# Four gated attention layers: two heads in each 64-row tile of TensorE, and value products unit by unit

## The reference

```
x = x + tanh(g_xattn[0]) * _L0_xattn_ref(_layernorm(x), ctx, ctx, ...)   # 16 heads of 8 features, biases
x = x + tanh(g_ffn[0])   * _L0_ffn_ref(_layernorm(x), ...)
x = x + tanh(g_xattn[1]) * _L1_xattn_ref(ctx, ctx, _layernorm(x), mask_Bx1xSxS2, ...)
...                                                                     # 16 heads, mask: z = where(mask == 0, -1e-20, z)
x = x + tanh(g_xattn[2]) * _L2_xattn_ref(...)                           # one head of 128 features
...
x = x + tanh(g_xattn[3]) * _L3_xattn_ref(..., mask_B, ...)              # 16 heads, only the first valid_len keys count
x = x + tanh(g_ffn[3])   * _L3_ffn_ref(_layernorm(x), ...)
```

## Time and profile before

| what | us |
| --- | --- |
| median of three runs | 6744.95 |
| the profiled execution | 6736.52 |
| its span, first to last instruction | 6734.7 |
| layer 0 attention: first product for a maximum, last update of `x` | 70.5, 1384.1 |
| layer 1 attention: last update of `x` | 3866.9 |
| layer 3 attention: last update of `x` | 6649.9 |
| TensorE busy, share of the span | 88% |

### The profile page before, as it was taken

The page is one execution under the profiler, slowest core; times in us unless marked ns, Lnnn a source line. Parts: engine busy times, 40 slices in busy tenths (PEclk is TensorE's granted clock), DMA queues, the critical chain, the costliest instruction groups (busy, mean ns, idle before and its releaser), DMA issues. The chain is left out here.

```text
span 6734.7 us, 123692 instructions
## 1 busy us (share of the span) xinstructions
PE 5947.1 (88%) x42776; PEld 4044.1 (60%) x42776; DVE 4732.6 (70%) x12652; ACT 3471.3 (52%) x5250; POOL 1972.7 (29%) x1415
## 2 busy tenths in 40 slices
PE   6999999969897999999999956768498799999996
PEld 4666666659894555555555545645388466566653
DVE  6878777867676666666666676634577777777775
ACT  3666666655553444444444433423255466666664
POOL 2222222224453222222222122334255222222220
PEclk9999999989997999999999977878699799999998
DMA  3333333220002333333333132356332333232321
GB/s 75 77 78 73 72 72 75 63 68 21 21 21 68 81 77 81 78 79 75 76 79 75 35 68 52 60 157 183 98 118 81 82 72 71 67 69 68 69 67 25
DMA packets 200964, 492.88 MB, mean 73 GB/s; under 512 B 31689, under 2 KB 135318, under 8 KB 199162
## 3 DMA queue, kind: packets, MB, share of 16 engines
q1 hardware_dynamic: 200386, 485.47, 29.5%
HBM read 270.18 MB, written 2.25 MB: 40 GB/s over the span
## 5 line engine op out<-in xcount | busy, mean ns | idle before, releaser
L850 PE MATMUL a_max<-a_stack,a_qblk 96*100 96x482 f32 (+1 forms) x4608 | 2003.5, 455 | 114.3 <-DVE a_mx L671 35.7
L550 ACT ACTIVATE a_probs<-a_scores 128x800 f32<-128x800 f32 (+1 forms) x1536 | 1281.3, 838 | 1019.0 <-PE a_scores L867 656.9
L863 PE MATMUL a_scores<-a_qblk,a_stack 128*128 128x400 f32 (+1 forms) x4608 | 1378.7, 372 | 8.1 <-POOL a_qblk L455 2.7
L665 DVE CUSTOM_DVE_ANT_0 a_dump<-a_max,a_mqf 100x482 f32<-100x482 f32 (+1 forms) x1536 | 978.5, 657 | 426.4 <-PE a_max L850 395.6
L850 PEld LDWEIGHTS a_max<-a_stack,a_qblk 96*100 96x100 f32 x4608 | 767.2, 167 | 745.1 <-issue 205.6
L671 DVE CUSTOM_DVE_ANT_0 a_dump<-a_max,a_penq 100x482 f32<-100x482 f32 (+1 forms) x1536 | 955.6, 657 | 280.9 <-PE a_max L850 261.7
L657 DVE TENSOR_REDUCE a_mx<-a_max 100x1 f32<-100x482 f32 (+1 forms) x1536 | 941.4, 654 | 257.6 <-PE a_max L850 239.8
L879 PE MATMUL a_pv<-a_probs,a_v_aug 128*32 128x200 f32 x18432 | 1051.8, 340 | 3.4 <-ACT a_probs L548 2.1
L863 PEld LDWEIGHTS a_scores<-a_qblk,a_stack 128*128 128x128 f32 (+1 forms) x4608 | 840.4, 186 | 185.6 <-issue 52.7
L1165 POOL TENSOR_TENSOR f_hb<-f_hb,f_wb 128x400 f32<-128x400 f32 x560 | 655.8, 1185 | 965.1 <-DVE f_hb L1413 490.2
L548 ACT ACTIVATE a_probs<-a_scores,a_kbias 128x800 f32<-128x800 f32 (+1 forms) x768 | 697.5, 926 | 413.6 <-PE a_scores L863 413.4
(11 more groups left out here) (302 smaller groups left out, 8471.7 us busy)
## 6 DMA issues: line engine op xcount, KB each, us to landing
a_stack<-a_khi SPq DMA_DIRECT2D x768, 180.5 KB, 3.4
a_ctxT<-in_ctxT_dram SPq DMA_DIRECT2D x128, 722.0 KB, 8.5
a_stack<-a_klo SPq DMA_DIRECT2D x384, 180.5 KB, 3.5
f_wb<-weights_by_token SPq DMA_DIRECT2D x24, 1600.0 KB, 10.7
f_wb<-weights_by_token SPq DMA_DIRECT2D x64, 400.0 KB, 6.3
a_ctxn<-in_ctxn_dram SPq DMA_DIRECT2D x32, 704.0 KB
a_mt_i<-in_mask1T_dram SPq DMA_DIRECT2D x32, 600.0 KB, 6.9
a_mq_i<-in_mask_dram SPq DMA_DIRECT2D x32, 564.1 KB
```

What stands on the lines that cost most here:

```text
L550: act.activation(out_, in_, ACT.Exp, scale=scale).then_inc(sc_free, 1)
L665: nc.vector.tensor_tensor_reduce(dump[:, k % 2, 0:n], src, mqf[:, b % 2, o:o + n], 1.0, -3.0e38, ALU.mult, ALU.max, out_).then_inc(mx_free, 1)
L850: pe.matmul(to[0:S, 0:n], qblk[0:96, b % 2, HALF * h + head, :], stack[0:96, b % 2, g, o:o + n], start=True, stop=True).then_inc(mx_full, 1)
L863: ins = pe.matmul(out_, stack[:, b % 2, 2 * h + g, kt * D:kt * D + r], qblk[:, b % 2, HALF * h + 4 * g:HALF * h + 4 * g + 4, :].rearrange( ...
```

## The change

The layout of keys and queries is new. `stack` and `qst` (in place of `qblk`) have four blocks of 32 rows. Two of them, rows 0 to 63 or 64 to 127, hold one half of the heads. A block of 32 rows is one head: rows 8 to 31 are its three parts of 8 features, rows 0 and 1 take minus the maximum in two parts, row 2 (layer 3) the penalty row for keys beyond the valid length, and the rest is ones against zeros. A product for a maximum now has 64 rows, and the scores of a unit are four products of 64 rows and 200 columns (two heads) in place of two of 128 rows and 400 columns.

`LEAD` is 24 units, one whole sample, and `half_of` swaps the halves on every second sample. So the maxima of sample b+1 and the scores of sample b always use different halves of the rows, and TensorE's list now alternates: one product for a maximum, two for scores, one for a maximum, two for scores, and then the value products of the unit before, each unit.

The key parts now go to memory (DRAM) with two DMAs a sample (`k_store`) and come back with eight. Four small DMAs a sample put the maxima into `qst` (`neg_load`). GpSimd makes the query parts with five instructions (`q_parts`) and the two parts of the maxima (`neg_parts`). In layer 3 the penalty per key is in the product, so that VectorE uses the plain reduction of layer 0 and ScalarE no bias. In layer 1 the two penalty products of a unit stand ahead of the maxima and scores. The query bias (layer 0) and a one in row 2 (layer 3) come from an added product of one row, `q_row`.

```diff
-LEAD = 16
+LEAD = UNITS
+ROWS = 32
...
+        SLOTS = 4
+        k_dram = nc.dram_tensor(f"{name}_k_parts", [SLOTS, 2, GROUPS, 2, 2, DK, KEYS], F32, kind="Internal").ap()
...
+        OUT_AT, NEG1_AT, CONCAT_AT, WO_AT, Q_AT, U_AT, NEG0_AT = 2, 4, 5, 8, 10, 13, 15
+        K0_AT, K12_AT, V01_AT, V2_AT = 1, 3, 7, 9
+        K0_FIRST, K12_FIRST, Q_FIRST, NEG_FIRST = 3, 6, 9, 14
...
+        def half_of(b, j):
+
+            return (b + j) % 2
...
+            def k_store(b):
...
+                for part, src in enumerate((khi, klo)):
+                    sp.dma_start(k_dram[b % SLOTS, :, :, :, part, :, :].rearrange("t g s i k -> (t g s) i k"),
+                                 src[:, :].bitcast(F32)).then_inc(k_out, 16)
...
+            def stack_load(b, j):
+                h = half_of(b, j)
+                sp.wait_ge(k_out, 32 * (b + 1))
+                scored(sp, b - 2, j)
+                if lens is not None and b == 0:
+                    sp.wait_ge(gone_out, 16)
+                for r in range(2):
+                    at, from_ = ROWS * (2 * h + r), k_dram[b % SLOTS, h, :, r]
+                    sp.dma_start(stack[at + 8:at + 24, b % 2, :, 0:KEYS].bitcast(F32),
+                                 from_.rearrange("g p i k -> (p i) g k")).then_inc(stack_in[b % 2][h], 16)
+                    sp.dma_start(stack[at + 24:at + 32, b % 2, :, 0:KEYS].bitcast(F32),
+                                 from_[:, 0].rearrange("g i k -> i g k")).then_inc(stack_in[b % 2][h], 16)
...
+            def neg_load(b, j):
+                h = half_of(b, j)
+                taken(sp, "neg", 2 * b + j)
+                for r in range(2):
+                    at = ROWS * (2 * h + r)
+                    sp.dma_start(qst[at:at + 2, b % 3, :, r, :].bitcast(F32), nsb[at:at + 2, :, :].bitcast(F32))\
+                      .then_inc(neg_in, 16)
...
+                act.activation(out_, in_, ACT.Exp, scale=scale).then_inc(sc_free, 1)
...
+            def q_parts(b):
+                taken(pool, "q", b)
+                scored(pool, b - 3, 1)
+                step(pool.tensor_copy(qh[:, :, :], qf[:, :, :]))
+                step(pool.tensor_scalar(ql[:, :, :], qh[:, :, :].bitcast(F32), low[:, 0:1], None, ALU.mult))
+                step(pool.tensor_tensor(ql[:, :, :], qf[:, :, :], ql[:, :, :], ALU.add))
+                for r in range(2):
+                    ins = pool.tensor_scalar(qst[:, b % 3, :, r, :], ql[:, :, :], low[:, 1 + r:2 + r], None, ALU.mult)
+                ins.then_inc(qst_ready, 1)
...
+            def neg_parts(b, j):
...
+                step(pool.tensor_copy(cols[:, :, :, 0], nm_))
+                pool.tensor_tensor(cols[:, :, :, 1], nm_, cols[:, :, :, 0].bitcast(F32),
...
+                nc.vector.tensor_copy(qf[:, :, :], p_ring("q", b)[:, 0:GROUPS * S].rearrange("p (g s) -> p g s", g=GROUPS))\
...
+                if mask is None:
                     nc.vector.tensor_reduce(out_, src, AX.X, ALU.max).then_inc(mx_free, 1)
                     return
...
+                reduce_ = nc.vector.tensor_reduce(nm[:, h, :], mx[:, h, :, :, :].rearrange("p g r c -> p (g r) c"), AX.X,
+                                                  ALU.max, negate=True)
+                reduce_.then_inc(nm_ready, 1)
...
+                nc.vector.tensor_copy(nsb[at:at + 2 * ROWS, :, :], p_ring("neg", 2 * b + j)[at:at + 2 * ROWS, 0:GROUPS * S]
+                                      .rearrange("p (g s) -> p g s", g=GROUPS)).then_inc(mx_free, 1)
...
-                    ins = pe.matmul(to[0:96, g * S:(g + 1) * S], wq[:, g, :], xnT[:, b * S:(b + 1) * S],
-                                    start=True, stop=True)
+                    ins = pe.matmul(to[:, g * S:(g + 1) * S], wq[:, g, :], xnT[:, b * S:(b + 1) * S],
+                                    start=True, stop=q_row is None)
+                    if q_row is not None:
+                        ins = pe.matmul(to[:, g * S:(g + 1) * S], q_row[:, g, :], ones_row[:, :], start=False, stop=True)
...
+                for g in range(GROUPS):
+                    ins = pe.matmul(to[at:at + 2 * ROWS, g * S:(g + 1) * S], nmsp[:, h, g, :].bitcast(F32),
+                                    ident[0:S, 0:S], start=True, stop=True)
+                ins.then_inc(mx_full, 1)
...
+                at = 2 * ROWS * half_of(b, j)
+                pe.matmul(to[0:S, 0:n], qst[at:at + 2 * ROWS, b % 3, g, r, :],
+                          stack[at:at + 2 * ROWS, b % 2, g, o:o + n], start=True, stop=True).then_inc(mx_full, 1)
...
+            def score_mm(b, u, g):
+                j, kt = divmod(u, KT)
+                if u % KT == 0 and g == 0:
+                    pe.wait_ge(neg_in, 32 * (2 * b + j + 1))
+                to = slot("exp", UNITS * b + u) if g == 0 and mask is None else p_slot("exp", UNITS * b + u)
+                at = 2 * ROWS * half_of(b, j)
+                ins = pe.matmul(to[:, g // 2, g % 2 * 2 * S:(g % 2 + 1) * 2 * S],
+                                stack[at:at + 2 * ROWS, b % 2, g, kt * D:(kt + 1) * D],
+                                qst[at:at + 2 * ROWS, b % 3, g, :, :].rearrange("p r s -> p (r s)"),
+                                start=mask is None, stop=mask is None or g % 2 == 1)
+                if g == GROUPS - 1:
+                    ins.then_inc(sc_full, 1)
...
+                for i in range(2):
+                    pe.matmul(to[:, i, 0:4 * S].rearrange("p (h s) -> p h s", h=4), identb[:, :],
+                              bc(pen[:, b % 2, u % KT, :], 1, 4), start=True, stop=False)
...
+                    if mask is not None:
+                        penalty_mm(b, u)
                     max_mm(2 * g)
-                    score_mm(b, u)
+                    score_mm(b, u, 0)
+                    score_mm(b, u, 1)
+                    max_mm(2 * g + 1)
+                    score_mm(b, u, 2)
+                    score_mm(b, u, 3)
                     if b > 0:
...
-                    max_mm(2 * g + 1)
-                    if u % 2 == 0 and (b > 0 or u > 0):
-                        for back in (2, 1):
-                            at = UNITS * b + u - back
-                            pv_mm(at // UNITS, at % UNITS)
+                    if b > 0 or u > 0:
+                        at = UNITS * b + u - 1
+                        pv_mm(at // UNITS, at % UNITS)
...
+        out = np.zeros(w.shape[:1] + (GROUPS, 4, 32), w.dtype)
+        for r in range(4):
+            for g in range(GROUPS):
+                n = HALF * (r // 2) + 2 * g + r % 2
+                head = w[:, DK * n:DK * n + DK]
+                out[:, g, r, 8:32] = np.tile(head, (1, 3))
+        return out.reshape(w.shape[:1] + (GROUPS, D))
```

372 lines of the change are left out of this document (165 added, 207 removed).

## The result

| | median | runs |
|---|---|---|
| before | 6740.3 us | 6734.5 to 6745.7 |
| after | 7052.3 us | 7025.5 to 7074.8 |

The changed kernel is slower: ratio 1.046, 95% interval 1.042 to 1.050. The forecast was 6780 us. 7052 lies in the range on record (6590 to 7120), but outside the forecast's own (to 6870), and between the forecast and rival 1; neither tells the cause. The profiled execution has a span of 7060.6 us at a mean clock of 0.884, 326 us over that of before.

What follows compares the result with a forecast made beforehand. TensorE was taken to bound all three attentions. From 6736.5 us, -35 in the steady part and +73 at the ends gave 6775 profiled, forecast as 6780; range 6590 to 7120, within full overlap 6690 to 6870.

Steps and rivals of the forecast that it cites:

- rival 1: Group of maxima and scores: halves overlap only in part, loads share one way in; 0.62 us, kernel 7115; chance 0.16.
- rivals 1 and 2: Group of maxima and scores: partial overlap (0.62 us, kernel 7115, chance 0.16) or none (0.87 us, 7690, chance 0.11).
- The terms of the unit: Layer 0 unit: maxima and scores 0.45, value products 0.34, changes of form 0.33; 1.12 us in place of 1.31.
- The waits before `neg_turn`: Layers 0 and 3: TensorE stands 0.6 us a sample, waiting for GpSimd's preparation behind the query parts.
- The clock falls: TensorE's clock drops as streaming covers 67% of a unit, before 87%; at 1.2 GHz everything nearly doubles; chance 0.03.
- 87%: Share of a unit covered by streaming in the kernel before, against 67% in the changed one.
- Everything would nearly double: Claimed effect on the kernel's times if TensorE's clock were at 1.2 GHz.
- +0.9, bounds 0 and 1.5: Layers 0 and 3, us a sample: TensorE waits 0.6 before `neg_turn` and 0.3 for late VectorE; bounds 0 and 1.5.
- 24 a layer: Both ends of each attention: 9.6 us for the longer lead, 7 for keys through memory, 7 at the end.
- The keys' way: Start of each attention: writing keys to memory and reading them back takes 14.6 us against 7.6; +7, bounds 5 and 12.
- 224 at most: Start of each attention: top DMA rate in GB/s for the keys, from 74 at a share of 0.33.
- +9.6: Start of each attention: lead of 24 units in place of 16, at 1.2 us a unit, costs 9.6 us more.

Runs made afterwards that it cites:

- e8: Changed kernel with halves in the same order every sample (no overlap), masked keys ahead of low key part, query numbers added by VectorE: 7285.6 us.
- e11: Changed kernel with masked keys first, query numbers added by VectorE, value products issued for two units together, VectorE reducing half the columns: 6403.3 us.
- e3: Changed kernel with all four one-row query products behind all four of 128 rows, in layers 0 and 3: 6859.0 us.
- e1: Changed kernel with GpSimd making the next sample's masked keys ahead of the low part of the keys: 6818.4 us.
- e2: Changed kernel without one-row query products in layers 0 and 3; VectorE adds the numbers while copying the projection out: 6792.0 us.
- e12: Kernel before, with a one-row product of zeros behind each of four query products in layers 0 and 3: 6875.8 us, ratio 1.020.
- pairs: Changed kernel with masked keys first and query numbers added by VectorE, plus value products issued for two units together every second unit: 6520.2 us.
- e7: Changed kernel with masked keys first and query numbers added by VectorE, plus both maxima of a unit ahead of its four scores: 6635.0 us.
- e4: Changed kernel with each half of the heads taken in the same order every sample, so nothing overlaps: 8937.9 us.

## Why the prediction was right in its range and wrong in its account

**Right by luck: the range and the sign.** The range reached to 7120 for rival 1, a partial overlap, which did not occur; a falling clock with a chance of 0.03, a wait of layer 1 that was no rival, and dearer starts filled it instead. "Slower" rested on 6775 against 6736.5, 38 us. Without the falls of layers 0 and 3 (142 us, below) and the wait of layer 1 (215) the same kernel would take about 7061 - 357 = 6704 us, some 31 under before, an estimate from the cadences: layer 0 undisturbed is 0.4 us a sample slower than before (41.0 against 40.6), but layer 3 is 1.9 faster and layer 1 4.0. The text's own sign of being wrong was a cadence of layer 0 outside 40 to 43; it is 43.04.

**Right in its mechanism.** The halves overlap in full: rivals 1 and 2 are out (0.63 with its change, against 1.02 in e8; maxima 0.22 apart with scores between, e11). Unit 1.10 (1.12), query projection 3.14 (3.2), changes 0.11 idle. The undisturbed sample of layer 0 takes 41.0 (41.3). The terms of the unit hold one by one: 0.44 for two maxima, 0.34 for the value products, and the two changes cost the remaining 0.32 (0.33), of which 0.08 is the load in the open ahead of the first maximum. e11's rows give the same price: half of it would be 0.16 a unit. Six changes less in e3 were 0.17 each (0.21).

**Right in sum only.** The waits before `neg_turn` are as long as forecast, 6.0 us in ten samples, but come in five turnings of 19 and end with VectorE, not GpSimd.

**Wrong: "The clock falls", 0.03.** I weighed only the mean share of streaming, and not with one measure: 87% counts distances of starts (1.14 of 1.31 us), by which the new unit has 0.79 of 1.12, 71% and not 67%. I asked nothing of the 3.1 us of alternating products that the same text prices. In 12 of 29 samples of layer 0 they bring 1.2 GHz for 13.7 to 17.1 us: (43.0 - 41.0) x 29 + (43.9 - 40.9) x 28 = 142 us (40.9 is the median cadence of layer 3 in e1). That the alternating stretch does it is shown by e2 and e3; that it takes the new kernel around it, by e12. "Everything would nearly double" was too dear: a fall costs about a third of its length.

**Wrong: the waits of layer 1.** I counted "+0.9, bounds 0 and 1.5" for layers 0 and 3 and only changes of form for layer 1. GpSimd's new order was in the diff, with a `k_low` of 3.2 us moved ahead of `gone_keys`; I did not follow ScalarE's queue behind it. Price (57.7 - 50.3) x 29 = 215 us, shown by e1 (234 with the start).

**Wrong the other way: layer 1 itself**, 50.3 undisturbed in place of 53.9: -104 us. Its unit is 1.55 us in e1, not 1.63 (1.9 a sample); the other 1.7 I cannot lay on one term.

**Wrong: the two ends.** "24 a layer", 73 in all, 50 of them for the starts. The starts cost 144. In layer 0 these are 46.5 us:
- The keys' way cost 14.6, above the bound of 12, since reading back took 15.1 where bandwidth and landing gave 6.5. The "224 at most" was worked out from other DMAs; with the engines over 90% busy these copies got 102 to 115 GB/s, and the other half's copies took part of that. No run held these back.
- The lead cost 50.45 - 24.01 = 26.4 more, where "+9.6" stands. I misread: 89.7 is ScalarE loading its table, not the end of the lead, which came at 94.5. Eight more units at the old pace would be 12.0. The other 14 hold 10.1 us of stands on DMAs, and the clock is at 1.2 GHz for all but 3.4 us of the new lead; why the clock stays low there was not tried.
- The remaining 5.5 fall in the first sample and were not followed.

The ends cost nothing, where 7 each was forecast: in layer 0 the last two updates and their samples take 54.2 us against 58.3, in all three layers 14 less than before. With the three samples of each layer that the cadences leave out, that is about 32 under the forecast.

These make 142 + 215 - 104 + 94 - 32, with -20 for base cadences 0.3 to 0.4 below the forecast in layers 0 and 3, = 295, for the 7060.6 - 6775 = 286 that were missed.

## What to carry to other kernels

Products whose forms alternate can cost more than their own time: here 3.1 us of them a sample were followed by 1.2 GHz for 13 us and more, while the same alternation in the kernel before was not. Keep such a stretch in one form (adding the numbers on VectorE took the cadence from an undisturbed 41.0 to 38.9). When you write an engine's queue in a new order, follow for each of its instructions who stands behind the waiting one on the next engine. And before removing work from the bounding engine, look up the second one and its buffers: pairs saved 65 us in place of 380, because the fourth maximum waits for one of three buffers and for VectorE's reduction of it (131 us with half the reading). With three such edits the same change gives 6520 us, 3.3% under the kernel before.

## What was not expected of the hardware

- Products in two halves of the rows start in another order than the program's: in e7 the third product starts 0.01 us behind the first and 0.30 ahead of the second. The Trainium skill ("TensorE: Matmul & The Clock Gate", Part 3) says that matmuls start and end in program order, without reordering; the rows of e7 disagree, for halves of the rows. The same part gives 3.07 times for four row tiles, which is 77% of full overlap. For two of 64 rows nothing is lost here: maxima on one half start 0.22 us apart with two scores on the other half between them (e11), as they did alone before.
- The same alternation of full and one-row products hardly costs the kernel before any clock (e12: 24 us low in layers 0 and 3 together), where after has 184 in layer 0 and 283 in layer 3, and e4, in which one half works at a time, 1242 in layer 0. Without the alternation one half at a time has none (e8).
- Eight instructions with one row of weights take as long as eight with 128 rows, 1.06 us with the way in (e3).
